# A gated linear attention layer with a sparse feed-forward: order of the small tile products, gates by tanh, and an earlier norm

## The reference, cut to what matters

```python
q = x @ Wq.T; k = x @ Wk.T; v = x @ Wv.T; gate = x @ Wg.T; beta = sigmoid(x @ Wb.T)
alpha = exp(-exp(A_log) * softplus(x @ Wa.T + dt_bias))
q = q / norm(q) / sqrt(DH); k = k / norm(k)
def step(S, inp):                        # S is 32x32 per head, token after token
    S = S * a_t
    delta = (v_t - k_t . S) * beta_t
    S = S + k_t (x) delta
    y_t = q_t . S
ctx = rmsnorm(ys, norm_w) * silu(gate)
attn = ctx @ Wo.T + bo
x = x + layernorm(attn(layernorm(x)))
```

## Time and profile before

| | us |
|---|---|
| median of 3 runs | 3423.63 |
| lowest, highest | 3423.21, 3427.54 |
| the profiled execution's own time | 3454.87 |
| its span, first to last instruction | 3453.1 |
| PE busy | 3006.9 (87% of the span) |
| DVE busy | 2357.6 (68%) |
| POOL busy | 1913.1 (55%) |
| ACT busy | 1824.4 (53%) |

### The profile page before, as it was taken

One profiled execution on the slowest core, in us unless ns is written; L12 is line 12 of the kernel. 1 busy time (PEld: TensorE's weight loads), 2 busy tenths in 40 slices (PEclk: granted clock), 3 DMA queues, 4 the chain that ended last, 5 costly groups with the idle time before them and its releaser, 6 DMA issues.

```text
span 3453.1 us, 141658 instructions
## 1 busy us (share of the span) xinstructions
PE 3006.9 (87%) x59368; PEld 2295.4 (66%) x59368; DVE 2357.6 (68%) x10708; ACT 1824.4 (53%) x4154; POOL 1913.1 (55%) x2903
## 2 busy tenths in 40 slices
PE   4899999999999999999999999999999999637774
PEld 4667777777777777777777777777777777414443
DVE  1667666666666766777666666666666677657896
ACT  2355555555555555555555555555555555326664
POOL 1555565455555555555565555555556555416887
PEclk9899999999999999999999999999999999759997
DMA  3544444544444445444444454444445444545773
GB/s 112 132 119 115 113 117 112 124 117 108 118 115 114 117 121 124 112 113 117 115 117 112 124 124 110 114 115 115 116 116 124 124 111 118 142 141 105 132 126 65
DMA packets 350030, 404.87 MB, mean 117 GB/s; under 512 B 31169, under 2 KB 293953, under 8 KB 348881
## 3 DMA queue, kind: packets, MB, share of 16 engines
q1 hardware_dynamic: 332752, 362.10, 42.1%
q0 software_dynamic: 16640, 33.71, 5.4%
HBM read 323.97 MB, written 75.93 MB: 116 GB/s over the span
## 4 chain that ended last, share of the span: by engine, by line
PE 62%; ACT 20%; DVE 11%; issue 4%; POOL 1%; ACTq 1%; DMA 1%; POOLq 0%; SPq 0%; DVEq 0%
PE work L437 25%; PE work L535 7%; PE work L543 3%; PE work L446 3%; DVE uk L1158 3%; DVE Ut L1155 3%; PE su L504 3%; PE work L454 2%; PE uq L497 2%; PE uk L477 2%; PE kkq L469 2%; PE uq L492 2%; PE work L530 2%; PE work L522 2%; PE work L511 2%
## 5 line engine op out<-in xcount | busy, mean ns | idle before, releaser
L437 PE MATMUL work<-xT,w_sb 128*128 128x256 f32 x5120 | 1314.1, 407 | 6.5 <-ACT beta L835 5.1
L992 POOL TENSOR_TENSOR pairs<-pairs,beta 128x240 f32<-128x240 f32 (+14 forms) x1920 | 862.4, 488 | 667.0 <-ACT beta L835 380.9
L437 PEld LDWEIGHTS work<-xT,w_sb 128*128 128x128 f32 x5120 | 996.3, 202 | 183.8 <-issue 31.1
L1158 DVE TENSOR_TENSOR uk<-uk,Ut 128x120 f32<-128x120 f32 (+14 forms) x3840 | 708.6, 226 | 1.1
L1155 DVE TENSOR_TENSOR Ut<-pairs,uk 128x120 f32<-128x120 f32 (+14 forms) x3840 | 688.2, 215 | 5.5 <-POOL pairs L992 5.0
L802 ACT ACTIVATE qraw<-work 128x512 f32<-128x512 f32 x128 | 75.9, 593 | 432.2 <-DVE kq L1171 305.5
L1165 DVE TENSOR_TENSOR S<-Sd,su 128x512 f32<-128x512 f32 x64 | 44.0, 687 | 359.1 <-PE su L504 359.1
L535 PE MATMUL work<-wo_sb,ctxT 128*128 128x512 f32 x512 | 240.6, 613 | 6.3 <-POOL ctxT L1011 6.3
L1003 POOL TENSOR_TENSOR kd<-kd,dec 128x512 f32<-128x512 f32 x64 | 68.0, 1084 | 258.8 <-DVE kd L1237 258.8
L492 PEld LDWEIGHTS uq<-kqd,S 32*32 32x32 f32 x8192 | 90.7, 114 | 156.8 <-ACT oT L792 105.8
L1145 DVE TENSOR_TENSOR uk<-vT,uk 128x128 f32<-128x128 f32 x256 | 62.9, 291 | 187.7 <-PE uk L485 115.8
(11 more groups left out here) (249 smaller groups left out, 5970.8 us busy)
## 6 DMA issues: line engine op xcount, KB each, us to landing
pairs<-pair_rows SPq DMA_DIRECT2D x512, 256.0 KB, 3.5
pairs<-pair_rows SPq DMA_DIRECT2D x512, 224.0 KB, 3.7
xt<-in_x SPq DMA_DIRECT2D x66, 256.0 KB, 5.4
pair_rows<-Ak SPq DMA_DIRECT2D x64, 256.0 KB, 2.3
x<-in_x SPq DMA_DIRECT2D x64, 256.0 KB, 4.8
out<-x SPq DMA_DIRECT2D x64, 256.0 KB, 3.7
wo_sb<-xs_rows SPq DMA_DIRECT2D x30, 258.0 KB, 2.9
w_sb<-in_w_in SPq DMA_DIRECT2D x1, 5120.0 KB, 14.9
```

Source lines behind the costliest of these rows:

```text
L437: mm = pe.matmul(w[:, half * BT:(half + 1) * BT], w_sb[:, f, j * D + hg * P:j * D + (hg + 1) * P], xT[:, f, :], start=(f == 0), stop=(f == ...
L992: ins = nc.gpsimd.tensor_tensor(a, a, beta[:, :, t:t + WID[t0]], ALU.mult)
L1158: link(v.tensor_tensor(uk[:, g, at + 1:at + 1 + n], uk[:, g, at + 1:at + 1 + n], Ut[:, g, 0:n], ALU.subtract), f"pairs_free{j}" if i and t ...
```

## The change

Five things change together.

1. **Whole batches.** `on_tiles` runs all 64 small products of a batch, and no batch is split. TensorE's `step` is written anew: the order has 12 whole batches, and between each two stand products that use the whole array. `chunk_to_outputs(1)`, which opened the next step, now ends its own.
2. **Gates by tanh.** Sigmoid(x) becomes 0.5 tanh(x/2) + 0.5: for beta two ScalarE instructions (Tanh, then Identity with scale and bias); for the gate ScalarE copies the bank to `silu`, takes the tanh from there, and VectorE makes (tanh + 1) times the copy; the factor 0.5 goes into `nw`. Tanh and Gelu are in one table set, loaded once a step by `load_tanh_gelu`; `load_ln_exp` follows once.
3. **Next tokens' norm half a step ahead.** `next_tokens_stats` on VectorE, `token_norm(x_rn, x_mv)` and `norm_tokens(xn, ...)` on ScalarE stand before the same work on `x1`, in the second half of the step before. SyncE loads the next tokens before `fetch_pairs(1, 1)`.
4. **Other orders.** ScalarE: `copy_outputs(0)` before the gate and norm work; `length_of_normed` in the next step. VectorE: the state is added right after the two rows of the output projection, the stats of them after it; `decay_products(0)` stands inside the last solve (after its second round). GpSimd: the decays' differences come before the rows' store, and the pairs' second half is split in two around the residual's addition.
5. **Buffers.** `qraw` and `sg` go: q and k are copied straight into `kq`; `qr` has four buffers; `gT` lies in `xn`, the gates' tanh in `y`. The banks' turn (`TURNS`) follows the new order, and `alpha` shares the logits' bank.

The diff, cut to its core:

```diff
 
 TURNS = [
-    ("logits",), ("xT", 0), ("xT", 1), ("qk", 0), ("rms", 0), ("rms", 1), ("alpha",), ("qk", 1), ("ss", 0),
-    ("qk", 2), ("wo", 0), ("wo", 1), ("rank",), ("ss", 1), ("G", 0), ("G", 1), ("qk", 3), ("ss", 2),
-    ("gate", 0), ("ss", 3), ("gate", 1), ("beta", 0), ("beta", 1), ("xfT", 0), ("xfT", 1), ("v", 0), ("v", 1),
-    ("hid",),
+    ("xT", 0), ("xT", 1), ("rms", 0), ("rms", 1), ("logits",), ("qk", 0), ("qk", 1), ("ss", 0), ("qk", 2), ("ss", 1),
+    ("G", 0), ("G", 1), ("wo", 0), ("wo", 1), ("rank",), ("ss", 2), ("qk", 3), ("gate", 0), ("ss", 3), ("gate", 1),
+    ("beta", 0), ("beta", 1), ("xfT", 0), ("xfT", 1), ("v", 0), ("hid",), ("v", 1),
...
-            def on_tiles(half, full, product):
-
-                for g in range(half * GU, (half + 1) * GU):
+            def on_tiles(product):
+
+                for g in range(G):
                     for h in range(HP):
                         mm = product(g, slice(DH * h, DH * h + DH), slice(DH * h, DH * h + CS))
-                if half and full:
-                    mm.then_inc(s[full], 1)
-
...
+            def state_to_outputs(c):
+
+                take(pe, "uq_free", free=1)
+                on_tiles(lambda g, q, q_half: pe.matmul(
                     uq[q, g], S[q, g, :], kqd[c][q, g, 1, :], start=(g == 0), stop=True, skip_group_check=True))
...
+                if after:
+                    take(pe, "ctx_ready", 2)
+                    output_projection(0)
+                if chain:
+                    change_state(0)
+                if after:
+                    output_projection(1)
+                if chain:
+                    state_to_u(1)
+                if late:
+                    ranks()
+                if ahead:
+                    squares_sum(2)
                     project("qk", 1, 1, 0)
-                if chain:
-                    state_to_u(1, 1)
-                if ahead:
                     project("qk", 1, 1, 1)
-                    squares_sum(2)
+                if chain:
+                    chunk_to_outputs(0)
+                if ahead:
                     project("gate", 4, 0, 0)
...
                 if after:
                     take(pe, "xf_ready", TB)
                     turn("xfT", xfw, 0)
-                if ahead:
-                    project("beta", 3, 1, 1)
-                if chain:
-                    state_to_outputs(1, 0)
-                if after:
                     turn("xfT", xfw, 1)
                 if ahead:
                     project("v", 2, 0, 0)
-                if chain:
-                    state_to_outputs(1, 1)
-                if ahead:
                     project("v", 2, 0, 1)
-                    project("v", 2, 1, 0)
-                if chain:
-                    change_state(1, 0)
                 if after:
                     take(pe, "xfT_ready", 2)
                     gate_hidden()
                 if chain:
-                    change_state(1, 1)
+                    change_state(1)
+                if ahead:
+                    project("v", 2, 1, 0)
+                if chain:
+                    chunk_to_outputs(1)
                 if ahead:
                     project("v", 2, 1, 1)
...
             def copy_and_square(n):
 
-                take(act, "kq_ready", free=2)
+                j, hp = divmod(n, 2)
                 take(act, "qk_full")
-                nc.scalar.activation(qraw[n % 2][:], bank("qk", n), ACT.Copy)
+                nc.scalar.activation(unit(kq, hp)[:, :, :, 1 - j, :], per_chunk(bank("qk", n)), ACT.Copy)
                 link(nc.scalar.activation(qsq[n % 2][:], bank("qk", n), ACT.Square), "q_sq_ready")
...
-            def sigmoid(name, hp, dst):
-                take(act, name + "_full")
-                return nc.scalar.activation(dst, bank(name, hp), ACT.Sigmoid)
+            def copy_gate(p, hp):
+
+                take(act, "gate_full")
+                link(nc.scalar.activation(flat(unit(silu[1 - p], hp)), bank("gate", hp), ACT.Copy), "gate_read", hold=True)
+
+            def gate_tanh(p, hp):
+
+                nc.scalar.activation(gate_t[hp], flat(unit(silu[1 - p], hp)), ACT.Tanh, scale=0.5).then_inc(s["gate_ready"], 1)
+
+            def beta_sigmoid(hp):
+
+                b = flat(unit(beta, hp))
+                take(act, "beta_full")
+                link(nc.scalar.activation(b, bank("beta", hp), ACT.Tanh, scale=0.5), "beta_read", hold=True)
+                link(nc.scalar.activation(b, b, ACT.Identity, scale=0.5, bias=half[:]), "beta_ready")
...
                     pair_decays(1)
-                    inverse_norm(2)
+                    copy_gate(p, 0)
                     inverse_norm(3)
-                    take(act, "gate_used", free=1)
-                    link(sigmoid("gate", 0, sg[:]), "gate_ready")
-                    take(act, "gate_used", free=1)
-                    link(sigmoid("gate", 1, sg[:]), "gate_ready")
+                    copy_gate(p, 1)
+                    take(act, "x_mv_ready")
+                    token_norm(x_rn, x_mv)
+                    norm_tokens(xn, xt, x_rn, "xn_ready")
                 if after:
                     take(act, "x1_mv_ready")
                     token_norm(x1_rn, x1_mv)
                     norm_tokens(xfw, x1, x1_rn, "xf_ready")
-                    length_of_normed(x1_mv, x1_rn)
-                if chain:
-                    copy_outputs(0)
-                if after:
-                    copy_turned("xfT", xfT, 0)
+                load_tanh_gelu()
                 if ahead:
                     if chain:
                         take(act, "vb_free")
-                    link(sigmoid("beta", 0, flat(unit(beta, 0))), "beta_ready")
-                    link(sigmoid("beta", 1, flat(unit(beta, 1))), "beta_ready")
+                        take(act, "pr_ready", 8)
+                    beta_sigmoid(0)
+                    beta_sigmoid(1)
+                    gate_tanh(p, 0)
+                    gate_tanh(p, 1)
+                if after:
+                    copy_turned("xfT", xfT, 0)
+                    copy_turned("xfT", xfT, 1)
+                if ahead:
                     copy_values(0)
...
+                    for hp in range(2):
+                        take(pool, "gT_ready")
+                        d = flat(unit(dec, hp))
+                        link(nc.gpsimd.tensor_tensor(d, d, gT[hp], ALU.subtract))
+                        by_chunk = d.rearrange("p (n t) -> p n t", t=C)
+                        link(nc.gpsimd.tensor_tensor(by_chunk, by_chunk, mask[:].unsqueeze(1).to_broadcast([P, GU * NC, C]), ALU.add),
+                             "diff_ready")
                 if late:
                     take(pool, "slot_ready")
...
+                for i, g in enumerate(turns):
+                    link(v.tensor_tensor(uk[:, g, h], uk[:, g, h], beta[:, g, th], ALU.mult),
+                         "vb_free" if i and (c, j) == (NC - 1, 1) else None, behind=1, hold=True)
 
                 for t0 in range(CS - 1):
+                    if t0 in between:
+                        between[t0]()
...
+            def output_rows(tb):
+
+                take(dve, "wo_full")
+                link(v.tensor_tensor(y[:, tb, :], bank("wo", tb), bo_sb[:], ALU.add), "wo_read", hold=True)
+
+            def gate_values(p, hp):
+
+                half_silu = flat(unit(silu[1 - p], hp))
+                take(dve, "gate_ready")
+                link(v.scalar_tensor_tensor(half_silu, gate_t[hp], 1.0, half_silu, ALU.add, ALU.mult), "gate_used")
...
+                if after:
+                    output_rows(0)
+                    output_rows(1)
+                if chain:
+                    add_to_state()
+                if ahead:
+                    for hp in range(2):
+                        take(dve, "g_copied")
+                        link(v.transpose(gT[hp], flat(unit(dec, hp))), "gT_ready")
...
                     take(dve, "dec_ready", 2)
+                if chain:
+                    take(dve, "corr_full")
+                    solve_half(1, 1, {2: lambda: decay_products(0)} if ahead else {})
+                elif ahead:
                     decay_products(0)
-                    take(dve, "gate_ready")
-                    link(v.tensor_tensor(flat(unit(silu[1 - p], 1)), bank("gate", 1), sg[:], ALU.mult), "gate_used")
-                    next_tokens_stats()
-                if chain:
-                    take(dve, "corr_full")
-                    solve_half(1, 1)
+                if ahead:
+                    gate_values(p, 0)
+                    gate_values(p, 1)
+                if chain:
                     add_to_state()
 
```

297 lines of the change are left out of this document (126 added, 171 removed).

## The result

The changed kernel takes 3477.14 us, median of four runs (3472.84 to 3480.50), against 3425.59 for the kernel before on the same chip: ratio 1.0148, interval 1.013 to 1.0166. It is 1.5% slower, well clear of the noise; 3282 was forecast, with 3190 to 3400 for eight cases in ten.

What follows compares the result with a forecast made beforehand. TensorE and its order were taken as the bound: 92.0 - 5.1 - 4.0 + 1.6 + 1.8 + 2.1 - 1.0 = 87.4 us a step, over 31 steps 3312, scaled by 0.991 to 3282 us. Eight-in-ten range: 3190 to 3400.

Steps and rivals of the forecast that it cites:

- What bounds the kernel: Whole step: TensorE, busy 84.8 of 92.0 us, sets the step, and its order decides.
- Waits that go: TensorE's waits for ScalarE (`uq` emptied, beta's bank, the next tokens' norm) disappear: gain 5.1 us a step.
- whole batches: On TensorE 24 half batches become 12 whole ones, saving ten splits: gain 4.0 us a step.
- A wait in the middle: `state_to_u(1)`, directly behind `output_projection(1)`, waits for VectorE to add bias and state: cost 1.6 us a step.
- The wait at the turning of `xf`: TensorE waits for the norm chain at the turning, then for beta's banks: cost 1.8 us a step, bounds 0 to 6.
- Issue stalls: Dense batches on TensorE wait for instruction blocks: 2.1 us a step more than the 1.0 of now.
- A: Rival: TensorE's instruction fetch never stalls; 3187 us, chance 0.13.
- C: Rival: slower than before, from 12 us of fetch stalls where one step ends and the next starts; 3586 us, chance 0.08.
- Clock: TensorE's slow clock costs 2.5 us a step; with shorter waits 1.0 of it comes back.
- The signs: Wrong if issue stalls exceed 8 us a step, the `xfw` wait exceeds 4, or 128-record batches take 1.9 behind projections.
- B: Rival: the norm chain through VectorE, GpSimd and ScalarE to `xfT` becomes the bound, 4 us a step; 3405 us, chance 0.15.
- D: Rival: ScalarE waits return under other names, new waits about eat the batches' gain; 3415 us, chance 0.04.

Runs made afterwards that it cites:

- after_mid: The changed kernel with the ranks and one sum of squares moved ahead of `state_to_u(1)`; 3467.81 us, ratio 1.0116 to the kernel before.
- after_spread: The changed kernel with skinny products (logits, alpha) set between projections of q and k instead of in a row; 3477.00 us, ratio 1.0074 to the kernel before.
- before_act: The kernel before with only ScalarE's order changed: chunk 0's outputs copied between the gate's sigmoids, normed length later, tables loaded; 3404.00 us, ratio 0.9923.
- after_all: The changed kernel with skinny products spread, `gate_hidden` at the step's end, state added before `output_rows(1)`, one scale later; 3403.69 us, ratio 0.9828 to the kernel before.
- all_early: after_all with the next tokens' statistics and norm earlier, x1's statistics ahead of the scales, `y`'s norm before qk 3's copy; 3226.37 us, ratio 0.9389.
- before_ahead: The kernel before with ScalarE reordered, `vb_free` early and whole batches, plus the next tokens' norm ahead of x1's; 3264.18 us, ratio 0.950, against 0.937 without that norm.
- after_light: The changed kernel with the pairs' DMAs carrying a quarter of their numbers, same instructions; 3416.78 us, ratio 0.997 to the kernel before.

## Why the prediction was wrong

*What bounds the kernel.* TensorE's order did, but not by itself. Behind its waits stood chains nearly as long as its own queue. The sum treated each wait as a price that is paid or not.

*Waits that go, whole batches.* Right: `oT` and `xn` are gone, beta's bank costs 1.1 a step (1.6 forecast), the work fell by 4.7 (4.0 forecast), the whole batch is 1.2.

*A wait in the middle.* Right to the tenth, 1.67 for 1.6. That nothing but idle time was behind it was wrong: after_mid removed it and gained 0.3%.

*The wait at the turning of `xf`.* Right in size, 2.1 for 1.8, and wrong in its making. I set VectorE's and ScalarE's path at 28.0 from the state's addition to the end of the norm, and TensorE's at 27.8. In the step shown they are 31.8 (1513.1 to 1544.9) and 33.3 (1513.2 to 1546.5), so `xf` is there before its turning; in five of ten steps it isn't, which makes the 0.94. The two sums were 3.8 and 5.5 too small, and that they missed the same way is luck. VectorE takes 24.9 for 21.2, most of it in the scales, 2.51 + 2.87 for 3.3, and ScalarE's part is right (6.9 for 6.8). In TensorE's queue the slow clock and the stalls fill the time.

*Issue stalls.* Right, 2.9 to 3.4 for 3.1, mostly at the places named. Rivals A and C were wrong in their mechanism: the stalls neither vanish nor reach 8. C alone, at 0.08, had the kernel slower than before; by the runs that is so for another reason than it gave.

*Clock.* **The term that failed.** I let 1.0 of 2.5 come back because the waits get shorter. By my own sum they don't: -5.1 + 1.6 + 1.8 + 2.1 is 0.4 more of idle time. The slow clock rose by 4.3, from 3.4 to 7.7. That is a miss of 5.3 out of 5.8 a step (+1.2 measured, -4.6 forecast); the gaps add 1.3, the work gives 0.7 back. Two things were left out. The clock is at 1.2 GHz also where TensorE is busy, over the run of logits, alpha and the first projection which the change has put in a row: 3.3 us a step are lost there and 0.8 in after_spread. And the clock is slow behind the new waits and stalls (1.5 behind the 1.90 at 1535.48; 1.7 a step behind the wait for `S`, 1.6 at the turning of `xf`). This is no fixed price: before_act has 2.0 less of gaps than before and 1.0 more of slow clock. The earlier trace rows had busy time at a slow clock in them: 17 us at 0.80, with 13.4 of them busy.

*The signs.* None of the three that were to show me wrong came up (stalls above 8, `xfw` above 4, batches of 1.9). The clock was to be above 0.94 and is 0.91 in the step shown; that was the sign of the term that failed, and it stood only among those for being right.

*The rivals.* B had 0.15 for a norm chain that adds 4 us. Its wait was 2.1 only while TensorE was itself slow. Once that was mended it was 4.1 + 1.0 (after_all), and with the chain shortened the step fell by 6.3 (all_early). So the forecast step of 87.4 can be had, and 84.75 too, with four faults mended at once: the run of small products, the dense end of the step, the late state add and the order of the norms. Without the third it is 88.6, without the fourth 91.0; without one of the first two it was not run. Alone these edits gave 0.7, 1.6, 0.8 and 1.3% (each ratio against 1.0148, from different calls, with intervals some 0.5% wide).

D, that ScalarE's waits come back under other names, is what before_act shows on the kernel before, and the reason why that edit alone gave so little there.

What stays open: which part of the shortened chain counts most (the order of the scales, `y`'s norm or the next tokens'; before_ahead has priced only the last), what besides the pairs' traffic makes instructions come late (after_light), and by what TensorE's clock decides between small products and gaps.

## What to carry to other kernels

When a wait is removed, ask which chain arrives next at the same place, and how late it could have come without being waited for: here four edits whose single gains sum to 4.4% are worth 7.5% together. Count a step on every engine's path with the clock and contention that its own rows show, and put nothing early into a queue in front of what the busiest engine is about to need. Judge a half clock by what runs (tiny and skinny products in a row) as well as by how long the engine waits.

## What the runs showed of the hardware

The scale of q and k takes 0.65 us at its shortest, 1.09 on average before and 1.42 after. The one at 1519.33 takes 2.51; GpSimd, in the same window:

```profile
1518.94 2.35 POOL L1019 TENSOR_TENSOR xfw<-xfw,pb_sb 128x1024 f32<-128x1024 f32 x1
```

GpSimd's instruction ends at 1521.29, and 1519.33 + 2.51 is 1521.84, 0.55 later, about what the scale takes alone: VectorE seems to have waited for all of it. The Trainium skill, page "SBUF — State Buffer", section "SBUF: two separate sides", says that a VectorE instruction with two inputs in SBUF and a GpSimd instruction that reads SBUF want the same port pair, that the first to start holds it for its whole length, and that the other one blocks. The trace agrees. In after_all three scales in a row took 5.85 (from 1595.94). It doesn't show as idle time: VectorE is called busy.

Eight products of 128x16 and eight of a projection, in all_early:

```profile
1542.50 0.96 PE L551 MATMUL work<-ceT,xfT 128*128 128x16 f32 x8
...
1544.65 1.97 PE L435 MATMUL work<-xT,w_sb 128*128 128x256 f32 x8
```

In after the same stand at 1572.91 and 1578.68 and take 1.66 and 3.76. The granted clock over the span is 0.946 in all_early and 0.907 in after, with the same instructions in another order; the slow clock is 3.0 and 7.7 us a step.

Of the "issue" stalls of TensorE above 0.4 us, 60 of 67 in after and 50 of 59 in all_early end 1.3 to 1.7 us after an instruction packet of q8 has ended.
